# All four quadrants for the first inverse product and for delta, with 26 block loads a pair: a gated-delta-rule layer on one core

## Time and profile before

| what | us |
|---|---|
| median of 3 runs | 813.8 |
| profiled execution, its own time | 817.35 |
| its span, first to last instruction | 815.2 |
| PE busy | 742.0 (91%) |
| DVE busy | 694.7 (85%) |
| ACT busy | 326.5 (40%) |
| POOL busy | 278.8 (34%) |

### The profile page before, as it was taken

One profiled execution on the slowest core, in us unless ns is written; L12 is line 12 of the kernel. 1 busy time (PEld: TensorE's weight loads), 2 busy tenths in 40 slices (PEclk: granted clock), 3 DMA queues, 4 the chain that ended last, 5 costly groups with the idle time before them and its releaser, 6 DMA issues.

```text
span 815.2 us, 26961 instructions
## 1 busy us (share of the span) xinstructions
PE 742.0 (91%) x11562; PEld 485.2 (60%) x11562; DVE 694.7 (85%) x1224; ACT 326.5 (40%) x737; POOL 278.8 (34%) x185
## 2 busy tenths in 40 slices
PE   1779989989899999999999999999999998989986
PEld 1535555756566565656566576666566565657664
DVE  4789998999899988998989988998988888887645
ACT  2235434444344345352534444353534362444120
POOL 3015411525252434325161424234252516234110
PEclk9979999999999999999999999999999999999979
DMA  7123050414242231404131231404123232312201
GB/s 223 58 65 88 24 99 24 91 37 71 64 85 50 36 99 27 101 10 84 56 80 42 46 95 22 106 15 82 40 38 98 29 105 29 73 21 31 42 2 53
DMA packets 140406, 49.79 MB, mean 61 GB/s; under 512 B 118144, under 2 KB 131840, under 8 KB 140160
## 3 DMA queue, kind: packets, MB, share of 16 engines
q1 hardware_dynamic: 139664, 47.93, 26.1%
q10 hardware_dynamic: 624, 0.15, 0.1%
HBM read 40.44 MB, written 7.60 MB: 59 GB/s over the span
## 4 chain that ended last, share of the span: by engine, by line
PE 54%; DVE 30%; issue 7%; ACT 4%; POOL 3%; DMA 1%; SPq 1%; DVEq 0%; ACTq 0%; POOLq 0%
PE bank L716 17%; DVE kq L259 11%; PE bank L737 4%; PE bank L807 4%; PE bank L916 4%; PE bank L836 3%; PE bank L803 3%; PE bank L864 3%; PE bank L805 3%; PE bank L744 2%; PE bank L767 2%; PE bank L849 2%; PE bank L819 1%; PE bank L943 1%; PE bank L780 1%
## 5 line engine op out<-in xcount | busy, mean ns | idle before, releaser
L716 PE MATMUL bank<-xnT,wq 128*128 128x512 f32 x512 | 254.3, 622 | 6.6 <-DVE kq L259 6.3
L259 DVE SCALAR_TENSOR_TENSOR kq<-bank,cw,kq 128x510 f32<-128x510 f32 (+2 forms) x288 | 213.6, 745 | 14.6 <-ACT kq L1044 7.7
L716 PEld LDWEIGHTS bank<-xnT,wq 128*128 128x128 f32 x512 | 89.8, 192 | 88.0 <-issue 71.2
L1044 ACT ACTIVATE kq<-bank,cw 128x512 f32<-128x512 f32 x96 | 65.9, 686 | 135.4 <-PE bank L716 132.3
L1232 POOL TENSOR_TENSOR Sd<-St,dec 128x256 f32<-128x256 f32 x32 | 20.8, 649 | 268.4 <-DVE St L383 218.7
L1226 POOL TENSOR_TENSOR kqg<-kq,rows 128x1024 f32<-128x1024 f32 x32 | 77.1, 2423 | 77.2 <-DVE kq L259 42.1
L1236 POOL TENSOR_TENSOR ost<-ost,cst 128x8 f32<-128x8 f32 x32 | 55.0, 1718 | 92.1 <-DVE ost L396 91.4
L916 PE MATMUL bank<-wo,oT 128*128 128x256 f32 x256 | 68.4, 384 | 0.1
L737 PE MATMUL bank<-xh,wguT 128*128 128x512 f32 x128 | 59.4, 607 | 1.6 <-DVE hf L271 1.6
L371 DVE TENSOR_TENSOR X<-UT,bank 128x256 f32<-128x256 f32 (+1 forms) x96 | 43.4, 461 | 17.5 <-PE bank L807 9.6
L916 PEld LDWEIGHTS bank<-wo,oT 128*128 128x128 f32 x256 | 45.9, 190 | 17.2 <-issue 12.1
(11 more groups left out here) (129 smaller groups left out, 1254.5 us busy)
## 6 DMA issues: line engine op xcount, KB each, us to landing
wq<-wqkvz_dram SPq DMA_DIRECT2D x16, 512.0 KB, 3.9
rows<-decay_rows SPq DMA_DIRECT2D x64, 128.0 KB, 3.0
rows<-decay_rows SPq DMA_DIRECT2D x32, 256.0 KB, 4.2
inverse_blocks<-UU SPq DMA_DIRECT2D x32, 128.0 KB
UT<-inverse_blocks SPq DMA_DIRECT2D x128, 32.0 KB, 2.4
wguT<-wgu_dram SPq DMA_DIRECT2D x8, 256.0 KB, 3.6
woraw<-wout_dram SPq DMA_DIRECT2D x16, 128.0 KB, 2.5
base_blocks<-ATP SPq DMA_DIRECT2D x128, 16.0 KB, 1.8
```

What stands on the lines that cost most here:

```text
L259: nc.vector.scalar_tensor_tensor(out=y[:, :, t:S], in0=p[:, :, 0:S - t], scalar=cw[:, m, i // 2, 3 - t:4 - t], in1=y[:, :, t:S], op0=ALU.m ...
L716: last = nc.tensor.matmul(ring[i % 2][:], wq[:, q, kc, i // 2, :], xnT[:, kc, (i % 2) * 512:(i % 2) * 512 + 512], start=kc == 0, stop=kc = ...
L1044: nc.scalar.activation(kq[:, i // 2, 2 * (i % 2):2 * (i % 2) + 2, :], split(ring[i % 2][:], 2), ACT.Copy, scale=cw[:, m, i // 2, 3:4]).the ...
```

## The change

- A second flip: for odd b and for b of 2 or 3 the side changes once each (`place2`), so that hz.0 and delta, too, use all four quadrants. `place` now goes by b % 2 instead of by half.
- hz.0 is one step with one semaphore for both halves, its 64 products in the order H, h inside i; it waits for the last `out` of two pairs before (`acc_done` m*4) instead of the last but one for its first half.
- delta writes to two banks; Y = nV + sums becomes two adds of 128 x 128 instead of one of 128 x 256.
- The blocks must lie on both sides now: uin has 26 DMAs instead of 10 (8 of 16 blocks each, the other 18 of 8 blocks each; before, 8 of 32 blocks and 2 of 16; a block is 16 rows of 64 bytes), with the same bytes.
- root's values for half 1 are copied to the other side by two small ACT copies a pair (`rt`).
- Every engine's list is new. In the middle: PE `6.out.3 8.ff 7.hz.0.0`; DVE `8.proj.2 6.state.1 8.proj.3 6.ks.2 6.norm.0 7.inv.2 6.state.2 6.gated.0 6.ks.3 8.proj.4 8.proj.5`. In pair 1 DVE has `2.proj.2` ahead of `1.inv.2`; for pair 0 `0.inv.0 0.inv.1 0.inv.2` stand before `1.gram.0 1.gram.1 1.proj.5`; for pair 15 `uout` stands before `14.fload` and `14.ff` before `15.hz`. SP has `bin` right behind `bout` in most pairs.

```diff
-        UIN = 16 * 10
+        UIN = 16 * 26
+        def place2(h, b):
+            return hs[h ^ b % 2 ^ b // 2]
# DVE, ks
-                    nc.vector.tensor_tensor(by_half(Y[:]), by_half(nV[:, q, chunk(c)]), sums(), ALU.add).then_inc(y_done, 1)
+                    for j, bs in enumerate((slice(0, 4, 3), slice(1, 3))):
+                        last = nc.vector.tensor_tensor(Y[:, bs], nV[:, q, chunk(c)][:, bs], split(CS[j][:, 0:2 * C], 2), ALU.add)
+                    last.then_inc(y_done, 1)
# SP, uin
-                            sp.dma_start(UT[at:at + BASE].rearrange("p k u c -> p (k u) c")[:, :, cols], dub[h, i].rearrange("k u r c -> r (k u) c")).then_inc(ui_in, 16)
-                        sp.dma_start(X[h * C:h * C + BASE, q, :, 0:BASE], dub[h, 0, 0].rearrange("u r c -> r u c")).then_inc(ui_in, 16)
+                            sp.dma_start(UT[at:at + BASE, 0].rearrange("p k u c -> p (k u) c")[:, :, cols], dub[h, i, 0].rearrange("k u r c -> r (k u) c")).then_inc(ui_in, 16)
+                            sp.dma_start(UT[at:at + BASE, 1, 0, :, cols], dub[1 - h, i, 1, 0].rearrange("u r c -> r u c")).then_inc(ui_in, 16)
+                            if i < NB - 1:
+                                sp.dma_start(UT[at:at + BASE, 1, 1, :, cols], dub[h, i, 1, 1].rearrange("u r c -> r u c")).then_inc(ui_in, 16)
+                        for H in range(2):
+                            sp.dma_start(X[h * C:h * C + BASE, q, half(H), 0:BASE], dub[h ^ H, 0, H, 0].rearrange("u r c -> r u c")).then_inc(ui_in, 16)
# PE, hz.0
+                    if j == 0:
+                        for i in range(HALF):
+                            for H in range(2):
+                                for h in range(2):
+                                    last = nc.tensor.matmul(M[H][hs[h ^ H], i * n:i * n + n], ATP[hs[h], q, H * HALF + i, 0, :], UT[hs[h], H, 1, i, 0:n],
+                                                            start=True, stop=True)
+                        last.then_inc(hz_ready, 1)
+                        return
# PE, delta
-                    for b in range(B):
+                    for b in (0, 2, 1, 3):
                         for h in range(2):
-                            u = b * NCH + c
-                            last = nc.tensor.matmul(CH[hs[h], 256 + b * C:256 + b * C + C], X[hs[h], q, u, :],
-                                                    Y[hs[h], b, :] if c else nV[hs[h], q, u, :], start=True, stop=True)
+                            u, n = b * NCH + c, b % 2
+                            last = nc.tensor.matmul(CS[b // 2][place(h, b), 256 + n * C:256 + n * C + C], X[place2(h, b), q, u, :],
+                                                    Y[place2(h, b), b, :] if c else nV[place2(h, b), q, u, :], start=True, stop=True)
# ACT, new
+                def root(m, q):
+                    wait(act, nv_done, m * 2)
+                    act.wait_ge(root_done, m + 1)
+                    for h in range(2):
+                        nc.scalar.activation(rt[hs[1 - h], :], stat[hs[h], 2, half(1)], ACT.Copy).then_inc(rt_done, 1)
```

More of the change, by code:

```diff
@@ L539, in _ @@
[L539 to L546, removed]
@@ L551, in _ @@
[L551 to L558, removed]
@@ L559, in _ @@
[L559 to L562, removed]
@@ L575, in _ @@
[L575 to L576 removed]
+                         "state": state, "norm": norm, "gated": gated, "turn": turn, "out": out, "fold": fold, "fo": fo}, """0.fold 0.proj.0 0.proj.1 0.proj.2 0.proj.3 0.e 0.stats 0.proj.4 0.proj.5 0.gram.0 0.gram.1 0.ff 0.gram.2 0.gram.3 1.e
@@ new lines, in _ @@
+                     0.gated.1 0.out.0 0.turn.1 2.gram.2 0.out.1 2.gram.3 1.vtr.0 0.out.2 1.vtr.1 0.out.3 3.proj.0 3.proj.1 1.hz.1.0
+                     1.hz.1.1 1.hz.2.0 1.hz.2.1 1.hz.3.0 3.e 1.hz.3.1 3.proj.2 3.proj.3 1.state.0 2.inv.0 1.ks.1 2.inv.1 1.state.1 3.proj.4
+                     1.ks.2 2.inv.2 1.state.2 1.norm.0 1.ks.3 3.stats 1.gated.0 3.proj.5 1.norm.1 3.gram.0 1.turn.0 3.gram.1 1.gated.1
+                     1.out.0 1.turn.1 1.out.1 2.vtr.0 1.out.2 2.vtr.1 3.gram.2 3.gram.3 1.out.3 4.proj.0 4.proj.1 2.hz.1.0 2.hz.1.1
@@ new lines, in _ @@
+                     4.inv.2 3.state.2 3.gated.0 3.ks.3 5.proj.4 5.proj.5 3.norm.1 3.turn.0 5.stats 3.gated.1 3.turn.1 3.out.0 3.out.1
+                     4.vtr.0 3.out.2 5.gram.0 5.gram.1 3.out.3 4.vtr.1 5.ff 5.gram.2 5.gram.3 4.hz.1.0 4.hz.1.1 4.hz.2.0 4.hz.2.1 4.hz.3.0
+                     6.e 4.hz.3.1 6.proj.0 6.proj.1 4.state.0 5.inv.0 4.ks.1 5.inv.1 6.proj.2 4.state.1 6.proj.3 4.ks.2 4.norm.0 5.inv.2
+                     4.state.2 4.gated.0 4.ks.3 6.proj.4 6.proj.5 4.norm.1 4.turn.0 6.stats 4.gated.1 4.turn.1 4.out.0 4.out.1 6.gram.0
@@ new lines, in _ @@
+                     6.gram.1 5.vtr.0 4.out.2 5.vtr.1 4.out.3 6.ff 6.gram.2 6.gram.3 5.hz.1.0 5.hz.1.1 5.hz.2.0 5.hz.2.1 5.hz.3.0 7.e
+                     5.hz.3.1 7.proj.0 7.proj.1 5.state.0 6.inv.0 5.ks.1 6.inv.1 5.state.1 7.proj.2 5.ks.2 7.proj.3 5.norm.0 6.inv.2
+                     5.state.2 5.gated.0 5.ks.3 7.proj.4 7.proj.5 5.norm.1 5.turn.0 5.gated.1 5.out.0 5.turn.1 5.out.1 7.stats 6.vtr.0
+                     5.out.2 6.vtr.1 7.gram.0 7.gram.1 5.out.3 7.ff 7.gram.2 7.gram.3 6.hz.1.0 6.hz.1.1 6.hz.2.0 6.hz.2.1 8.e 6.hz.3.0
@@ new lines, in _ @@
+                     6.hz.3.1 8.proj.0 8.proj.1 6.state.0 7.inv.0 6.ks.1 7.inv.1 8.proj.2 6.state.1 8.proj.3 6.ks.2 6.norm.0 7.inv.2
+                     6.state.2 6.gated.0 6.ks.3 8.proj.4 8.proj.5 6.norm.1 6.turn.0 8.stats 6.gated.1 6.turn.1 6.out.0 6.out.1 7.vtr.0
+                     6.out.2 8.gram.0 7.vtr.1 8.gram.1 6.out.3 8.ff 8.gram.2 8.gram.3 7.hz.1.0 7.hz.1.1 7.hz.2.0 7.hz.2.1 7.hz.3.0 9.e
+                     7.hz.3.1 9.proj.0 9.proj.1 7.state.0 8.inv.0 7.ks.1 8.inv.1 9.proj.2 7.state.1 9.proj.3 7.ks.2 7.norm.0 8.inv.2
@@ new lines, in _ @@
+                     7.state.2 7.gated.0 7.ks.3 9.proj.4 9.proj.5 7.norm.1 7.turn.0 8.vtr.0 7.gated.1 7.out.0 7.turn.1 7.out.1 9.stats
+                     7.out.2 8.vtr.1 9.gram.0 9.gram.1 7.out.3 9.ff 9.gram.2 9.gram.3 8.hz.1.0 8.hz.1.1 8.hz.2.0 8.hz.2.1 10.e 8.hz.3.0
+                     8.hz.3.1 10.proj.0 10.proj.1 8.state.0 9.inv.0 8.ks.1 9.inv.1 8.state.1 10.proj.2 8.ks.2 8.norm.0 10.proj.3 9.inv.2
+                     8.state.2 8.gated.0 8.ks.3 10.proj.4 10.proj.5 8.norm.1 8.turn.0 10.stats 8.gated.1 9.vtr.0 8.turn.1 8.out.0 8.out.1
@@ L588, in _ @@
+                     15.ks.1 15.state.1 15.ks.2 14.fo.0 15.state.2 15.ks.3 15.norm.0 15.gated.0 15.ff 15.norm.1 15.turn.0 14.fo.1
+                     15.gated.1 15.out.0 15.fo.0 15.turn.1 15.out.1 15.fo.1 15.out.2 15.out.3""")
                 dve.wait_ge(acc_done, PAIRS * 4)
```

383 lines of the change are left out of this document (190 added, 193 removed).

## The result

The changed kernel takes **853.25 us** (median of four runs, 849.12 to 858.57) against 814.54 (813.3 to 816.93) for the kernel before beside it: ratio 1.0475, 95% interval 1.0394 to 1.0556. It is slower, as forecast, but by 39 us and not by 12.5. Medians, ranges and ratios in this document are of fast runs; one run, of stored_old, was 1.8% longer than the fastest of its kernel and is left out.

A forecast was written before the change was run, and what follows sets the result against it. PE, 97% busy, was taken to set the pace; with late loads outweighing its gain, the terms over all pairs summed to +12.5 us, 829.9 for the profiled execution, a median of 826.3 us, range 800 to 838.

The forecast's parts named there:

- What PE gains: Delta and hz.0 on PE in four quadrants: 0.88 and 0.3 us a pair, together 1.2, 19 us in all.
- What the loads cost: 26 load issues on SP at 0.50 us each: loads end 8.4 us later after their first issue (7.4 to 9.9).
- What the new order gives back: DVE's inv.2 moves ahead of state.2, ks.3, gated.0 and proj.4: starts 3.8 us earlier in pair 10.
- What ACT pays: Two small copies a pair, and Q copies delayed about 0.8 us by hz.0's one semaphore: counted as nothing.
- What DVE pays: Y as two adds on the serial chain: 0.08 to 0.15 us more, 48 times, 4 to 7 us.
- loads stay hidden: Rival: loads land before PE reaches hz.0, at 0.43 us a step or less; PE keeps its gain, 799 us; chance 0.25.
- long issues: Rival: every uin meets a long issue on SP, another 1.2 us at some 14 pairs, 843 us; chance 0.06.

The follow-up runs named there:

- stored_old: Changed kernel with the old lists, the flip done when the inverse's blocks are stored, ten loads a pair: 831.5 us, ratio 1.0195.
- oldorder10: Changed kernel with the lists of the kernel before and ten loads a pair (half of the inverse's blocks wrong): 826.2 us.
- neworder10: Changed kernel under its own new lists with ten loads a pair (half of the inverse's blocks wrong): 841.6 us, ratio 1.0313.
- late_waits: Kernel before with only the two new waits, at hz.0 (both halves reporting together) and turn.0: 838.2 us, ratio 1.0301.

## Why the prediction was wrong

**The step that failed** is the one under *What PE gains*: "PE would then reach hz.0 of pair 10 at about 560.0", that is, that PE by itself becomes 1.2 us a pair faster and only the loads can hold it. With no late load at all it becomes slower: from one hz.0 to the next are 46.0 us in the kernel before, 46.6 in oldorder10 and 47.2 in neworder10, where 44.8 would have been right. Two terms were put at nothing: the new waits of hz.0 and turn.0, and what the new order takes from the serial chain. That the kernel came out slower, as forecast, is in part luck: the 2.1 us of waiting for loads that were to make it so in the middle pairs is not there. Term by term:

- *What PE gains*: delta's 0.22 us right; hz.0 sized at 0.3 us, 0.88 measured, the bound that I had named for a halving. 28 us and not 19, in the kernel's favour.
- *What the loads cost*: the issue time, the landing and the 13 us right. Their price is 12 us in the kernel after, by taking them away. But the mechanism, "hz.0 comes 0.9 us later than before, and PE waits 2.1 us for the loads" in pairs 4 to 11, failed: of these only pair 11 waits for them (1.5 us), and in pair 8 they land 0.3 us ahead of hz.0. PE arrives late by itself.
- *What the new order gives back*: wrong by a term. inv.2 does come earlier (it ends 27.9 us after hz.0 of the pair before, mean of pairs 5 to 10, and not 31.8). I booked that and nothing for what inv.2 and the proj steps were moved past: state.2, ks.2, state.1, gated on the serial chain. PE stands there. The order alone costs 41 us on the old arithmetic, 15 with the quadrants and ten loads.
- *What ACT pays* and *what PE gains*: Q's late copies were costed at nothing because gram.1 lies over them, 0.8 a pair without it; the wait of hz.0 for the last accumulation and that of turn.0 for the last d were not in the sum at all. Alone they are 17 and 7 us, and eat most of the quadrants' gain. Both stand in the kernels (acc_done `m * 4`, d_done `m * 4 + 4`), the first also in the description of the change.
- *What DVE pays*: Y's 4 to 7 us right (4), the one cost on the chain that I had.
- The clock was in no term. 15 us of PE's busy time I put down to it, more than the loads are worth.
- Rivals: *loads stay hidden* was half true (they are, in most middle pairs) and PE did not keep its gain, so its 799 was no nearer; *long issues* (843) came nearest, for a wrong reason: PE waits 5.8 us for loads in all.

The ledger of the quadrants under the old lists: -28 (PE's work) +25 (two waits) +4 (Y) +8 (clock, 0.983 to 0.971 by the fitted line) = +9; measured +12 (8 to 17). The 25 and the 4 hold what the clock cost in their own runs (late_waits ran at 0.974 to 0.985), so some of the 8 may be counted twice; the fit of the sum is no proof of its parts. Open stays how the new order's 15 us divide among its moves: the one group tried gave nothing, and mixtures of the two orders were not tried on the chip.

## What to carry to other kernels

Price a faster step by what it newly waits for: read every changed wait and bank in the diff, and put the wait alone into the old kernel to see its cost. A written-out order that makes room for one long step takes it from the serial chain; list what each moved step is moved past on every engine. Where TensorE gets new waits, as here from 97% busy to 90%, count the clock that it loses besides the gaps.
